# Gathered rows divided into three bf16 parts on chip, and summed by twelve bf16 products a chunk, in five walks over the edges of a graph network

## What is computed

```python
support_t = jax.ops.segment_sum(xt[s], r, num_segments=N_NODES)       # layer 0
out = jax.ops.segment_sum(h[s] * norm[:, None], d, num_segments=n)    # layer 3, twice
```

## Time and profile before

| | us |
|---|---|
| median of 3 runs | 9434.25 |
| lowest, highest | 9422.37, 9440.75 |
| span of the profiled execution | 11044.3 |
| busy in it: TensorE, weight loads | 4003.0, 3408.2 |
| busy in it: VectorE, ScalarE, GpSimd | 3958.5, 1410.5, 5820.6 |

### The profile page before, as it was taken

The page is one execution under the profiler, slowest core; times in us unless marked ns, Lnnn a source line. Parts: engine busy times, 40 slices in busy tenths (PEclk is TensorE's granted clock), DMA queues, the critical chain, the costliest instruction groups (busy, mean ns, idle before and its releaser), DMA issues. The chain is left out here.

```text
span 11044.3 us, 116200 instructions
## 1 busy us (share of the span) xinstructions
PE 4003.0 (36%) x18072; PEld 3408.2 (31%) x18073; DVE 3958.5 (36%) x9685; ACT 1410.5 (13%) x3057; POOL 5820.6 (53%) x5941
## 2 busy tenths in 40 slices
PE   1333423333345554321033443333333333333332
PEld 1333323333335552010033333333323333233332
DVE  5335664444445557920011111111122222422224
ACT  1000011111124445710000000000000000000000
POOL 0667744555430003777766666666645565356664
PEclk6555556666665555555556665555555555555555
DMA  1111103333332221000011111111111111111111
GB/s 42 43 42 42 44 25 92 93 90 91 89 88 81 81 81 36 1 21 21 7 54 52 53 53 47 42 42 43 43 39 40 41 42 42 35 41 42 42 43 41
DMA packets 364720, 548.58 MB, mean 50 GB/s; under 512 B 124102, under 2 KB 217114, under 8 KB 364650
## 3 DMA queue, kind: packets, MB, share of 16 engines
q0 software_dynamic: 186368, 330.08, 11.1%
q1 hardware_dynamic: 148330, 190.56, 5.6%
q10 hardware_dynamic: 29952, 27.28, 1.0%
HBM read 448.36 MB, written 99.13 MB: 50 GB/s over the span
## 5 line engine op out<-in xcount | busy, mean ns | idle before, releaser
L658 PE MATMUL PS<-GATHERED,OH 128*128 128x128 f32 (+1 forms) x10240 | 2403.2, 416 | 4359.3 <-issue 1547.1
L658 PEld LDWEIGHTS PS<-GATHERED,OH 128*128 128x128 f32 x10240 | 2145.9, 312 | 4664.6 <-issue 2130.2
L550 POOL DMA_INDIRECT GATHERED<-row_tab,IDX x2496 | 2464.6, 987 | 1899.6 <-issue 1030.8
L550 POOL DMA_INDIRECT GATHERED<-gat_tab,IDX x832 | 784.8, 943 | 898.4 <-DVEq L1505 509.8
L575 POOL DMA_INDIRECT list_dram<-REC_NOW,PLACE_NOW x832 | 912.5, 1097 | 313.8 <-issue 258.4
L550 POOL DMA_INDIRECT GATHERED<-typed_b_tab,IDX x832 | 817.9, 983 | 483.1 <-issue 241.0
L550 POOL DMA_INDIRECT GATHERED<-typed_tab,IDX x832 | 808.9, 972 | 479.6 <-issue 234.8
L715 PE MATMUL PS<-IDENT,GATHERED 128*128 128x128 f32 x3328 | 588.1, 355 | 968.6 <-DVEq L1505 823.1
L1220 DVE TENSOR_TENSOR X<-X,PS 128x128 f32 x512 | 146.6, 286 | 2013.7 <-remote 1305.8
L715 PEld LDWEIGHTS PS<-IDENT,GATHERED 128*128 128x128 f32 x3328 | 544.3, 188 | 1012.4 <-issue 1010.5
L1204 DVE TENSOR_SCALAR OH<-IOTA,DSTF,WF 128x128 f32 x2048 | 601.1, 361 | 678.5 <-issue 648.1
(11 more groups left out here) (243 smaller groups left out, 3912.5 us busy)
## 6 DMA issues: line engine op xcount, KB each, us to landing
gat_rows<-GATHERED SPq DMA_DIRECT2D x208, 264.0 KB
GATHERED<-gat_rows SPq DMA_DIRECT2D x208, 264.0 KB, 2.8
GATHERED<-row_tab,IDX POOLq DMA_INDIRECT x2496
ROWI<-dst_rows ACTq DMA_DIRECT2D x208, 128.0 KB
ROWI<-dst_rows SPq DMA_DIRECT2D x208, 128.0 KB
GATHERED<-gat_tab,IDX POOLq DMA_INDIRECT x832
list_dram<-REC_NOW,PLACE_NOW POOLq DMA_INDIRECT x832
GATHERED<-typed_tab,IDX POOLq DMA_INDIRECT x832
```

The lines of the kernel that those rows point to most:

```text
L550: pool.indirect_dma_start(out=rows, out_offset=None, in_=table, in_offset=bass.IndirectOffsetOnAxis(ap=IDX[:, k:k + 1], axis=0),).then_inc ...
L658: last = mm(bank(p)[:, 0:r.shape[1]], onehot(p, t), r, start=(t == 0), stop=(t == CT - 1))
```

## The change

In the five walks the gathered f32 rows are divided into three bf16 parts whose sum is the row, in a new tile `PARTS` of two buffers (u mod 2). ACT copies the high part out of the row (`part_hi`), DVE subtracts it from the row in place (`part_rest`), ACT copies the middle part (`part_mid`), and DVE subtracts that and writes the low part, with which the slot in GATHERED is free (`wk.free`); the buffer of parts is free after the add (`parts_free`). The one-hots are bf16 and hold no weights; each product of f32 becomes three of bf16 on the same one-hot. In l3a and l3b DVE multiplies the rows in place by the edge weights ahead of the division (`row_weighed`). In l0 the weights themselves are divided once (`WP`, in T) and ACT copies the three parts into column D. The tables of blocks hold uint16 in rows of 8 instead of int32 in rows of 4. Several semaphores are shared by the walks, with offsets of `splits * NCH`. Walk gb keeps its f32 form (`exact`).

```diff
-    REGS = 4
+    REGS, ROW = 4, 8
+    SEC = D + 2
-        RANGES = sb("RANGES", [1, REGS * NCH], I32)
+        RANGES = sb("RANGES", [1, ROW * NCH], U16)
+        OHB = OH[:, :].bitcast(BF16)
+        PARTS = sb("PARTS", [P, 2 * CT * NP3 * SEC], BF16)
+        WP = T[:, 0:NT * NP3 // 2].bitcast(BF16)
+        def parts_of(u, width=D):
+            a = PARTS[:, (u % 2) * CT * NP3 * SEC:(u % 2 + 1) * CT * NP3 * SEC]
+            return a.rearrange("p (t k f) -> p k t f", t=CT, k=NP3)[:, :, :, 0:width]
+        def rows_of(u):
+            return G3[:, u * CT:(u + 1) * CT, 0:D]
...
                 for t in range(CT):
-                    r = rows(t)
-                    last = mm(bank(p)[:, 0:r.shape[1]], onehot(p, t), r, start=(t == 0), stop=(t == CT - 1))
+                    for n, r in enumerate(rows(t)):
+                        last = mm(bank(p)[:, 0:r.shape[1]], onehot(p, t, 1, r.dtype == F32), r, start=(t == 0 and n == 0),
+                                  stop=(t == CT - 1 and n == len(rows(t)) - 1))
...
+            def split_rows(name):
+                return lambda i, u: hold(pe, walks[name].free, RING * i + (RING + 1 + u))
...
+                def chunk(i, u, last_):
+                    c = RING * i + u
+                    hold(act, wk.gathered[u], 16 * CT * (i + (wk.rounds * NIT + 1)))
+                    if not last_:
+                        next_indices(wk, column, i, u)
+                    hold(act, parts_free, c + (wk.splits * NCH + 1))
+                    if weighed:
+                        hold(act, row_weighed, c + ((wk.rounds - 1) * NCH + 1))
+                    nc.scalar.activation(parts_of(u)[:, 0, :, :], rows_of(u), ACT.Copy).then_inc(part_hi, 1)
+                    if weights:
+                        nc.scalar.activation(parts_of(u, D + 1)[:, :, :, D],
+                                             WP[:, bass.ds(c * (CT * NP3), CT * NP3)].rearrange("p (t k) -> p k t", k=NP3),
+                                             ACT.Copy).then_inc(weight_kept, 1)
+                    hold(act, part_rest, c + (wk.splits * NCH + 1))
+                    nc.scalar.activation(parts_of(u)[:, 1, :, :], rows_of(u), ACT.Copy).then_inc(part_mid, 1)
...
+                def weigh_rows(i, c, u):
+                    hold(dve, wk.gathered[u], 16 * CT * (i + (wk.rounds * NIT + 1)))
+                    v.tensor_tensor(rows_of(u), rows_of(u), per_edge(weights, c, D), ALU.mult).then_inc(row_weighed, 1)
+                def rest(c, u):
+                    hold(dve, part_hi, c + (wk.splits * NCH + 1))
+                    v.tensor_tensor(rows_of(u), rows_of(u), parts_of(u)[:, 0, :, :], ALU.subtract).then_inc(part_rest, 1)
+                def low(c, u):
+                    hold(dve, part_mid, c + (wk.splits * NCH + 1))
+                    v.tensor_tensor(parts_of(u)[:, 2, :, :], rows_of(u), parts_of(u)[:, 1, :, :],
+                                    ALU.subtract).then_inc(wk.free, 1)
...
-                            onehots(c + 1, block_values((u + 1) % sets)[2], 1 - p, weights, column).then_inc(wk.onehot, 1)
+                            if not exact:
+                                if weights is not None:
+                                    weigh_rows(i + (1 if u == RING - 1 else 0), c + 1, (u + 1) % RING)
+                                rest(c + 1, (u + 1) % RING)
+                            onehots(c + 1, block_values((u + 1) % sets)[2], 1 - p, column, exact).then_inc(wk.onehot, 1)
+                            if not exact:
+                                low(c + 1, (u + 1) % RING)
...
-                        dve.nop(nofuse=True).then_inc(wk.free, 1)
+                        if exact:
+                            dve.nop(nofuse=True).then_inc(wk.free, 1)
+                        else:
+                            dve.nop(nofuse=True).then_inc(parts_free, 1)
...
+            dve.wait_ge(s_stored, 16)
+            split(WF[:, :], WREST, [WP.rearrange("p (t k) -> p k t", k=NP3)[:, k, :] for k in range(NP3)])
             dve.sem_inc(counted, 1)
+            dve.sem_inc(w_split, 1)
+            dve.sem_inc(parts_free, 2)
```

More of the change, by code:

```diff
@@ L240, in __init__ @@
                 self.more_added = sem(f"more_added_{n}")
[L242 to L246, removed]
+        walk_l0 = Walk("l0")
+        walks = {"l0": walk_l0, "g1": Walk("g1", adds=False), "ga": Walk("ga", gathers=False, adds=False),
+                 "gb": Walk("gb", gathers=False), "l2": Walk("l2", splits=1, like=walk_l0)}
+        walks["l3a"] = Walk("l3a", rounds=1, gathered=walks["l0"].gathered, splits=3, like=walk_l0)
+        walks["l3b"] = Walk("l3b", rounds=2, gathered=walks["l0"].gathered, splits=4, like=walk_l0)
+        walks["l2b"] = Walk("l2b", rounds=1, gathered=walks["l2"].gathered, splits=2, like=walk_l0)
+        part_hi, part_rest, part_mid, parts_free = (sem(f"part_{k}") for k in ("hi", "rest", "mid", "free"))
+        row_weighed = sem("row_weighed")
         row_in = [sem(f"row_in_{u}") for u in range(RING)]
@@ L845, in indices @@
                     start += n
+                for u in range(RING):
+                    chunk(NIT - 1, u, True)
             for req in requests["before_l0"]:
@@ L851, in _ @@
                 answer(*req)
-            wk = walks["l0"]
-            first_indices(wk, SRCF)
-            def weights_beside(i, last_):
-                for u in range(RING):
-                    c = RING * i + u
-                    hold(act, wk.gathered[u], 16 * CT * (i + 1))
-                    nc.scalar.activation(G3[:, u * CT:(u + 1) * CT, D], WF[:, bass.ds(c * CT, CT)],
-                                         ACT.Copy).then_inc(weight_kept, 1)
-                    if not last_:
-                        next_indices(wk, SRCF, i, u)
-            with act.Fori(0, NIT - 1) as i:
-                weights_beside(i, False)
-            weights_beside(NIT - 1, True)
+            act.wait_ge(w_split, 1)
+            indices("l0", weights=True)
             for req in requests["l0_sums"]:
@@ L1024, in _ @@
             dense(dn, denses["l3a"], 4)
-            indices("l3a")
+            indices("l3a", weighed=True)
             for req in requests["l3a"]:
@@ L1028, in _ @@
             dense(dn, denses["l3b"], 5)
-            indices("l3b")
+            indices("l3b", weighed=True)
             for req in requests["l3b"]:
@@ L1216, in aggregate @@
                 wk = walks[name]
+                exact = ahead is not None
                 def add(b, p):
```

82 lines of the change are left out of this document (43 added, 39 removed).

## The result

The changed kernel takes 10216.97 us (median of 4 runs, 10216.05 to 10220.57), the kernel before 9435.38 us beside it: ratio 1.0831, 95% interval 1.0815 to 1.0846. It is slower by 782 us, where the forecast had 560 (9990) and the range 9430 to 10480. One thing is needed to read the numbers: the kernel before took 9431 to 9445 us in four jobs and 11015 us in a fifth, and the profiled execution of the earlier trace rows, 11044 us, is of that second, disturbed kind, so every ratio here is to runs of the kernel before in the same job, and stages are compared between profiles of one kind.

The account below looks back on a forecast made before the run. Unprofiled walks were taken to run near the floor of GpSimd's gathers, 1039 us. Terms 64 (l2) + 54 (l2b) + 2 x 152 (l3a, l3b) + 118 (l0) + 20 (ends) = +560 on 9434 gave 9990 us, range 9430 to 10480.

Parts of the forecast that it names:

- rival 3: Walks: 0.19 us contention per operation, POOL and DVE holding each other up; +886, so 10320 us; chance 0.22.
- (f): Ends and tables: weight division +5, last chunks of walks +15; uint16 table loads bounded by 0 and -143 us, taken as 0.
- (c): Division: hidden in l2; in l3a and l3b VectorE with ScalarE handovers takes 5.7 us a chunk against POOL's 5.0, 1194 a walk.
- (d): Gather walks: added two-input VectorE operations hold up gathers, 0.13 us each; l2 +64, l2b +54, l3 floor +114.
- these crawls: VectorE control instructions slow now and then in gather walks, one branch up to 730 ns; claimed to come only from profiling.
- The 1610 us: Profiled span over unprofiled median; with real crawls it would have to be missing from 3060 us outside walks and g1.
- (a): TensorE in the walks: a sum becomes 12 bf16 products, taken as 1.9 us, bounds 1.4 and 2.8; worth 0 on the path.
- (b): One-hots in bf16: in l3a and l3b four TENSOR_SCALARs (1.11 us) become one TENSOR_TENSOR of 0.69; no gain from smaller output.
- rival 4: Walks: every TENSOR_TENSOR holds a gather for its whole 0.69 us; over 11400 us; chance 0.02.
- (e): l0, where VectorE also ranks edges: first half +27 by contention, second half +91 by VectorE's work; +118 us.
- (g): Early release of the gather slot: worth 0 where POOL doesn't wait, something in the profiled execution with its 970 us of waits.
- Rival 1: Crawls are real in every run and slots bound the walks, so early release gains: 9250 us; chance 0.14.

Follow-up runs that it names:

- e9: Kernel before with uint16 tables and the one-hots of l0, l2 and l2b made by one-input TENSOR_SCALARs, on an undisturbed chip: 9521.06 us, ratio 1.0096.
- e1: Kernel before with only the tables of blocks changed to uint16, in the job where the kernel before took 11015 us: 11202.25 us, ratio 1.0162.
- e6: Changed kernel with only the high part's product, 4 products a sum instead of 12, division kept whole: 10166.62 us, ratio 1.0778 to the kernel before.
- e7: Changed kernel with the multiplication by edge weights done one chunk earlier, same instructions in other order: 10065.62 us, ratio 1.0672 to the kernel before.
- e10: Kernel before with uint16 tables and two extra TENSOR_TENSORs a chunk in l2b, l3a, l3b, both inputs in SBUF, undisturbed chip: 9814.4 us, ratio 1.0405.
- e11: Kernel before with uint16 tables and two extra TENSOR_TENSORs a chunk in l2b, l3a, l3b, second input in PSUM, undisturbed chip: 9553.37 us, ratio 1.0129.
- e3: The same kernel as e10, in the job where the kernel before took 11015 us: 11073.03 us, ratio 1.005.
- e4: The same kernel as e11, in the job where the kernel before took 11015 us: 11286.54 us, ratio 1.025.

## Why the prediction was right, and where it was off

**The number.** 10217 lies in the range of 9430 to 10480, but above the 9800 to 10200 given to the forecast itself, and nearer to rival 3's 10320 than to 9990. By its stages rival 3 doesn't hold: it had 228 us for each of l3a and l3b (measured 172 and 173), 105 for l2 (65) and 200 for l0 (106), and nothing for the tables. More than half of what the sum lacked is the term under (f); the mechanism under (c) and (d) is the one that the experiments show.

**What bounds the kernel.** The conclusion held, the reason for it did not. Undisturbed walks but l0 stand at POOL's floor of 1039 us: 1041 to 1045 in e9. But "I take these crawls as the profile's own" was wrong. The 1610 us between the profiled execution and the median compared two kinds of execution, not a profiled one with an unprofiled one: in e1's job the kernel before took 11015 us in the timed runs. The argument "1610 us would have to be missing outside the walks" only excluded that the runs at 9434 had the crawls, and that is all that the forecast needed. For the same reason the profile of the changed kernel, forecast at 11000 to 11600 us, came out at 10215.5: it was taken where nothing crawls.

**(a) TensorE, 0 on the path.** Right as to the sum of the walks: e6 gave back 52 us. It hides 80 us that l3 gained and 50 that l2 and l2b lost. A sum takes 1.46 us, at the lower bound of 1.4; a view of one chunk of l3b in the changed kernel (other rows left out):

```profile
9504.12 0.28 DVE L1224 TENSOR_TENSOR T<-T,PS 128x128 f32 x1
9505.70 0.69 DVE L1228 TENSOR_TENSOR GATHERED<-GATHERED,WF 128x512 f32<-128x512 f32 x1 [1.30 <-issue]
9505.88 1.46 PE L655 MATMUL PS<-PARTS,OH 128*128 128x128 bf16 x12 [4.08 <-issue]
9506.49 0.63 ACT L847 ACTIVATE PARTS<-GATHERED 128x512 bf16<-128x512 f32 x1 [2.98 <-DVE GATHERED L1228]
9507.22 0.69 DVE L1232 TENSOR_TENSOR GATHERED<-GATHERED,PARTS 128x512 f32<-128x512 f32 x1 [0.83 <-ACT PARTS L847]
9507.83 0.72 DVE L1207 TENSOR_TENSOR OH<-IOTA,DSTF 128x512 bf16 x1
9508.01 0.63 ACT L853 ACTIVATE PARTS<-GATHERED 128x512 bf16<-128x512 f32 x1 [0.89 <-DVE GATHERED L1232]
9508.74 0.69 DVE L1236 TENSOR_TENSOR PARTS<-GATHERED,PARTS 128x512 bf16<-128x512 f32 x1 [0.19 <-ACT PARTS L853]
9509.35 0.28 DVE L1224 TENSOR_TENSOR T<-T,PS 128x128 f32 x1
```

**(b) One-hots.** 0.69 to 0.72 us in bf16, as taken.

**(c) The division.** From add to add are 5.23 us (9504.12 to 9509.35; the median of the walk is 5.21), forecast 5.0 (3.3 + 1.7) without the second blocks. From the add to the first operation it is 1.58 us instead of 1.0, as the load of the table stands there with 0.95; ScalarE's copies took 0.63 instead of 0.72, which gives back 0.2. So the tables' new type, priced at nothing under (f), stands in the chain of l3 too, with 0.6 us a chunk; as e7's walks, at POOL's pace, are only 65 to 72 us shorter, my estimate is that int32 tables could give back up to that much in each of l3a and l3b. No run has the changed kernel with int32 tables. That these handovers bind in l3 is shown by e7: with one of them gone the walk is 65 us shorter and POOL's pace ends it. 1194 us were forecast for l3, 1216 measured. VectorE's busy time there was forecast at over 700 us and is 635: 880 x 0.69 + 256 x 0.28 = 679 is all that the operations could have made, and in the rows neighbours overlap (the one of 9507.22 ends after 9507.83). The time above it is handovers and control.

**(d) Contention.** Its place and direction held (e10, e11), and the forecast for l2 was met. As a price per operation 0.13 us was a term of the wrong kind. Divided through, l2 pays 83 / 672 = 0.12, l2b 119 / 672 = 0.18, l3a 86 / 880 = 0.10, and e10 over e11 0.07 in l2b and 0.28 in l3a. What is paid hangs on how often a gather begins inside an operation, and that on how the two engines' rhythms lie to each other: 379 of 832 in l2b, 398 in l3a, but late in the operation there. l2b's +95 instead of +54 is this term. Rival 3 had 0.19 for all, which fits l2b and not the others; rival 4's whole 0.69 fits none.

**(e) l0.** 118 forecast, 106 measured. The second half is slower than the first, as forecast, but by less. Two windows of l0, split at the start of the 417th of its 832 gathers:

```profile
271.00:850.00 579.00, 182.85 (x1500) 152.93 (x1500) 334.21 (x560) 162.46 (x412) 452.33 (x416) 0.50 0.18 47
850.00:1523.00 673.00, 186.07 (x1523) 155.19 (x1524) 493.10 (x688) 153.53 (x407) 491.40 (x417) 0.50 0.16 41
```

The halves take 579 and 673 us, where the forecast had 520 + 17 + 27 = 564 and 697. In e11 they take 535 and 611, where it had 537 and 606 for the kernel before. So the first half grew by 44 us instead of 27 and the second by 62 instead of 91: two errors that nearly cancel, which is luck.

**(f) Tables and ends.** The step that failed. The tables' uint16 loads were bounded by 0 and -143 us, with no reason that excluded a loss; e11 is 122 us over the kernel before, and gb, where no gather's pace covers the loads, alone is 135 longer. "Four registers are read as before" counted registers and not the time of a load. This term is 122 of the 222 us by which the forecast fell short. The rest is, roughly, l2b with 41, l3a and l3b with 41 together and the ends, 54 us instead of 20, less 12 in l0.

**(g) Early release.** Nothing was seen of it in undisturbed executions, where the old form's POOL waited 4 to 16 us for slots in each of l2, l2b, l3a and l3b, and 33 in l0 (e11). What it does where control instructions crawl was not run for the changed kernel. Rival 1 stays untested there, and whether the change would gain or lose on such a chip is open, as is what makes the instructions crawl: the same kernel had it in one job and not in another, and among kernels of one job the time did not follow the work (e3 below e1).

## What to carry to other kernels

A walk that is paced by GpSimd's gathers isn't free room for VectorE: an operation with two inputs in SBUF costs by the gathers that begin beside it, while one with a PSUM input or a scalar operand costs next to nothing (e11, e9), so count starts that fall inside, not operations. Look first whether the profiled execution is of the same kind as the timed ones, by a stage that the change doesn't touch. And price every change of type of a small table that registers are loaded from, in the stage where nothing covers the load.

## What the runs showed of the hardware that I had not expected

- Four registers loaded from a uint16 table take 0.95 us, from an int32 table 0.34.
- In the changed kernel, a gather that begins inside a VectorE operation with two SBUF inputs is longer by about the rest of the operation less 0.12 us (0.47 for 0.59, 0.27 for 0.39); one that has begun before the operation loses nothing (290 gathers, mean 0.00). Ahead of e10's pairs of such operations 37 gathers of l3a that began up to 0.2 us before lost 1.12 us each on average.
- The same kernel takes 11255 or 9553 us (e4 and e11, profiled spans) on two chips, with equal busy times of the engines in l3a; control instructions of up to 1.4 us come with it.
- ScalarE copies 128x512 from f32 to bf16 in 0.63 us, where the int16 form of the earlier trace rows takes 0.72.
